# A four-layer graph network: layer-norm statistics made where rows are finished, high parts on GpSimd, GRU gates in fp16 parts, and two tests in place of nested ones

## Time and profile before

| | us |
|---|---|
| median of 3 runs | 3095.23 (3094.25 to 3100.11) |
| profiled execution | 3090.32 |
| its span, first to last instruction | 3088.6 |

### The profile page before, as it was taken

One profiled execution on the slowest core, in us unless ns is written; L12 is line 12 of the kernel. 1 busy time (PEld: TensorE's weight loads), 2 busy tenths in 40 slices (PEclk: granted clock), 3 DMA queues, 4 the chain that ended last, 5 costly groups with the idle time before them and its releaser, 6 DMA issues. The chain is left out here.

```text
span 3088.6 us, 44367 instructions
## 1 busy us (share of the span) xinstructions
PE 2345.9 (76%) x14134; PEld 1718.8 (56%) x14134; DVE 1944.9 (63%) x4750; ACT 1263.5 (41%) x2067; POOL 545.7 (18%) x1539
## 2 busy tenths in 40 slices
PE   3499999759455999987834975779545299999999
PEld 2377777558323877776512754657444144444458
DVE  5467667433437777776238778887883677777741
ACT  4455655231346666661256754667412200000000
POOL 0000000000014444340025543445300000000000
PEclk9699999879777999998956987889877599999999
DMA  1322122035100000000100000000003000000013
GB/s 44 115 94 94 73 90 75 5 127 196 43 16 6 23 24 19 25 23 16 44 17 5 15 11 10 11 15 16 10 10 111 40 1 0 0 0 0 0 48 93
DMA packets 49249, 120.82 MB, mean 39 GB/s; under 512 B 5904, under 2 KB 24624, under 8 KB 45744
## 3 DMA queue, kind: packets, MB, share of 16 engines
q1 hardware_dynamic: 49072, 118.83, 11.5%
HBM read 93.85 MB, written 24.97 MB: 38 GB/s over the span
## 5 line engine op out<-in xcount | busy, mean ns | idle before, releaser
L1823 DVE SCALAR_TENSOR_TENSOR fil_acc<-bank,fil_node,fil_acc 128x256 f32<-128x256 f32 x682 | 329.9, 484 | 110.3 <-PE bank L1891 97.6
L1285 PE MATMUL bank<-idf,X 128*128 128x128 f32 x968 | 137.1, 304 | 215.7 <-DVE step_recips L1750 215.7
L1362 ACT ACTIVATE step_PT<-bank 128x512 f32<-128x512 f32 (+1 forms) x264 | 128.2, 574 | 380.5 <-PE bank L1285 380.1
L1889 PE MATMUL bank<-parts_in,fil_xTh 128*128 128x512 f16 x704 | 268.3, 381 | 0.0
L1890 PE MATMUL bank<-parts_in,fil_xTh 128*128 128x512 f16 x704 | 268.0, 381 | 0.0
L1891 PE MATMUL bank<-parts_in,fil_xTl 128*128 128x512 f16 x704 | 267.8, 380 | 0.0
L1295 PE MATMUL bank<-kH,qHL 128*128 128x512 f16 (+1 forms) x264 | 104.4, 396 | 193.4 <-ACT step_E L1371 149.3
L1285 PEld LDWEIGHTS bank<-idf,X 128*128 128x128 f32 x968 | 121.5, 156 | 227.6 <-DVE step_recips L1750 219.1
L672 PE MATMUL bank<-V,HL 128*128 128x256 f32 x968 | 236.7, 386 | 0.2
L1317 PE MATMUL bank<-H,step_PT 128*128 128x256 f32 x968 | 216.0, 379 | 0.0
L1317 PE MATMUL bank<-A,step_PT 128*128 128x256 f32 x968 | 216.0, 379 | 0.0
(11 more groups left out here) (365 smaller groups left out, 5061.1 us busy)
## 6 DMA issues: line engine op xcount, KB each, us to landing
gat_A<-in_adj SPq DMA_DIRECT2D x22, 1408.0 KB, 6.0
step_a<-adjT SPq DMA_DIRECT2D x44, 352.0 KB, 3.0
gcn_raw<-in_L_W SPq DMA_DIRECT2D x16, 512.0 KB, 4.8
split<-gcn_halves SPq DMA_DIRECT2D x16, 512.0 KB, 3.4
parts_in<-split SPq DMA_DIRECT2D x4, 2048.0 KB, 19.4
adjT<-gat_a SPq DMA_DIRECT2D x22, 352.0 KB, 2.2
gcn_a<-adjT SPq DMA_DIRECT2D x22, 352.0 KB, 3.9
out_a<-adjT SPq DMA_DIRECT2D x22, 352.0 KB, 3.0
```

The costliest lines, as they stand in the source:

```text
L1285: last = pe.transpose(p_bank[n % nb][:, i * 128:i * 128 + 128], M[j][:, (b + i) * 128:(b + i) * 128 + 128], core.idf[:])
L1362: act.activation(PT[:, b * 128:(b + m) * 128], p_bank[n % len(p_bank)][:, 0:m * 128], ACT.Copy).then_inc(pT_done, 1)
L1823: c(dve.scalar_tensor_tensor(out=acc[k][:], in0=ps, scalar=node[k][:, n:n + 1], in1=acc[k][:], op0=ALU.mult, op1=ALU.add))
L1889: pe.matmul(w_bank[n % 4][:], xTh[k][:, x], wh[:, blk], start=c == 0, stop=False)
```

## The change

- x comes by four transfers, and ln0 makes the statistics of a quarter as soon as it is there.
- Statistics live in one tile for all norms. Those for ln1 are made in the attention stage behind each updated tile, those for ln2 in the graph convolution, those for ln2b (19 of 22) at the end of step 1, those for ln3 in ln2b.
- The high part is made by GpSimd from H and a column `by`, the low part by VectorE in one operation from H, `by` and the high part; the small buffers go.
- In ln2b, GpSimd adds the shift b to x ahead of VectorE, which scales, adds and makes the statistic for ln3.
- The gate weights and the features are split into fp16 high and low parts; each float32 product becomes three fp16 products (high by high, low by high, high by low), scaled by 64 and scaled back where the biases are added.
- `settle` makes one test for a repair (once at most) and then one test for the ties, side by side instead of nested.

The diff, cut to its core:

```diff
+LOADS = 4
+SG = 64.0
...
-AGAIN = 2
...
+        self.stats = sb("stats", [128, T * 6])
+        self.x_loaded = [ctx.enter_context(nc.semaphore(f"x_loaded{n}")) for n in range(LOADS)]
...
-        x_loaded = nc.alloc_semaphore("x_loaded")
...
-            sp.dma_start(core.X[:].rearrange("p (t f) -> p t f", t=T),
-                         x.rearrange("(t p) f -> p t f", p=128)).then_inc(x_loaded, 16)
-            sp.wait_ge(x_loaded, 16)
+            for n in range(LOADS):
+                part = slice(T * n // LOADS, T * (n + 1) // LOADS)
+                sp.dma_start(core.X[:].rearrange("p (t f) -> p t f", t=T)[:, part, :],
+                             x.rearrange("(t p) f -> p t f", p=128)[:, part, :]).then_inc(core.x_loaded[n], 16)
...
-        stats = sb("stats", [128, T * 6])
+        stats = core.stats
...
-        u = [sb(f"u{k}", [128, D]) for k in range(2)]
+        by = sb("by", [128, T])
...
-            def statistics(t, k):
-                dve.bn_stats(cols(stats, t, 6), cols(src, t)).then_inc(sem["stats_done"], 1)
-
-            pipelined(dve, [(0, statistics)])
-            dve.wait_ge(sem["stats_done"], T)
+            if parts:
+                if scale_rows is None:
+                    dve.memset(by[:], SH).then_inc(sem["by_ready"], 1)
+                else:
+                    dve.tensor_scalar(by[:], scale_rows[:], SH, None, ALU.mult).then_inc(sem["by_ready"], 1)
+                dve.wait_ge(sem["by_ready"], 1)
+            for n in range(LOADS):
+                if loading:
+                    dve.wait_ge(core.x_loaded[n], 16)
+                for t in range(max(counted, T * n // LOADS), T * (n + 1) // LOADS):
+                    dve.bn_stats(cols(stats, t, 6), cols(src, t)).then_inc(sem["stats_done"], 1)
+            if counted < T:
+                dve.wait_ge(sem["stats_done"], T - counted)
...
-            def split(t, k):
-                reuse(dve, sem["lo_done"], t)
-                dve.wait_ge(sem["rows_done"], t + 1)
-                if scale_rows is None:
-                    dve.tensor_scalar(u[k][:], cols(H, t), SH, None, ALU.mult).then_inc(sem["scaled"], 1)
-                else:
-                    dve.tensor_scalar(u[k][:], cols(H, t), cols(scale_rows, t, 1), SH,
-                                      ALU.mult, ALU.mult).then_inc(sem["scaled"], 1)
-
             def low(t, k):
                 dve.wait_ge(sem["hi_done"], t + 1)
-                dve.tensor_tensor(lo(HL, t), u[k][:], hi(HL, t), ALU.subtract).then_inc(sem["lo_done"], 1)
+                dve.scalar_tensor_tensor(out=lo(HL, t), in0=cols(H, t), scalar=cols(by, t, 1), in1=hi(HL, t),
+                                         op0=ALU.mult, op1=ALU.subtract)
 
             def scale_and_add(t, k):
                 dve.wait_ge(sem["rows_done"], t + 1)
-                c = Chain(dve, sem["affine_steps"], t * 2)
-                c(dve.tensor_tensor(cols(H, t), cols(H, t), gb[0][:], ALU.mult))
-                c(dve.tensor_tensor(cols(H, t), cols(H, t), gb[1][:], ALU.add))
-                dve.tensor_tensor(cols(X, t), cols(X, t), cols(H, t), ALU.add)
+                dve.wait_ge(sem["shifted"], t + 1)
+                dve.tensor_tensor(cols(H, t), cols(H, t), gb[0][:], ALU.mult).then_inc(sem["affine_steps"], 1)
+                dve.wait_ge(sem["affine_steps"], t + 1)
+                dve.tensor_tensor(cols(X, t), cols(X, t), cols(H, t), ALU.add).then_inc(sem["added"], 1)
+
+            def count(t, k):
+                dve.wait_ge(sem["added"], t + 1)
+                dve.bn_stats(cols(stats, t, 6), cols(X, t)).then_inc(sem["x_counted"], 1)
 
             if affine:
                 dve.wait_ge(sem["affine_loaded"], 48)
-                pipelined(dve, [(0, scale_and_add)])
+                dve.wait_ge(sem["aggregated"], T)
+                pipelined(dve, [(0, scale_and_add), (1, count)])
+                dve.wait_ge(sem["x_counted"], T)
             if parts:
-                pipelined(dve, [(0, split), (1, low)])
+                pipelined(dve, [(0, low)])
+
+        if affine:
+            @block.gpsimd
+            def _(pool):
+                pool.wait_ge(sem["affine_loaded"], 48)
+
+                def shift(t, k):
+                    pool.tensor_tensor(cols(X, t), cols(X, t), gb[1][:], ALU.add).then_inc(sem["shifted"], 1)
+
+                pipelined(pool, [(0, shift)])
+
+        if parts:
+            @block.gpsimd
+            def _(pool):
+                pool.wait_ge(sem["by_ready"], 1)
+
+                def high(t, k):
+                    pool.wait_ge(sem["rows_done"], t + 1)
+                    pool.tensor_scalar(hi(HL, t), cols(H, t), cols(by, t, 1), None, ALU.mult).then_inc(sem["hi_done"], 1)
+
+                unrolled(pool, [(0, high)])
...
-            def high(t, k):
-                act.wait_ge(sem["scaled"], t + 1)
-                core.fence(act)
-                act.activation(hi(HL, t), u[k][:], ACT.Copy).then_inc(sem["hi_done"], 1)
-
-            pipelined(act, [(0, rows), (1, high)] if parts else [(0, rows)])
+            pipelined(act, [(0, rows)])
...
-        wih, whh = sb("wih", [128, 6 * D]), sb("whh", [128, 6 * D])
+        weight_parts = [[sb(f"{n}{part}", [128, 6 * D], F16) for part in "HL"] for n in ("wih", "whh")]
...
-        xT = [sb(f"xT{k}", [128, 2 * D]) for k in range(2)]
+        xH, xL = ([sb(f"x{part}{k}", [128, 2 * D], F16) for k in range(2)] for part in "HL")
+        weights = [E2[:, 0:6 * D], P[1][:, 0:6 * D]]
...
+            for i, (whole, (high, low)) in enumerate(zip(weights, weight_parts)):
+                dve.wait_ge(w_high, i + 1)
+                dve.scalar_tensor_tensor(out=low[:], in0=whole, scalar=SG, in1=high[:], op0=ALU.mult,
+                                         op1=ALU.subtract).then_inc(w_low, 1)
+            dve.wait_ge(w_low, 2)
...
+            def low_features(t, k):
+                dve.wait_ge(xT_ready, t + 1)
+                dve.tensor_tensor(xL[k][:], xt_bank[:], xH[k][:], ALU.subtract).then_inc(xL_ready, 1)
...
-                dve.tensor_tensor(rz[k][:], rz_bank[:], bi[:, 0:2 * D], ALU.add).then_inc(gates_read, 1)
-                dve.tensor_tensor(inn[k][:], n_bank[:, 0:D], bi[:, 2 * D:], ALU.add).then_inc(gates_read, 1)
-                dve.tensor_tensor(hn[k][:], n_bank[:, D:], bh[:, 2 * D:], ALU.add).then_inc(gates_read, 1)
+                dve.scalar_tensor_tensor(out=rz[k][:], in0=rz_bank[:], scalar=1 / SG, in1=bi[:, 0:2 * D], op0=ALU.mult,
+                                         op1=ALU.add).then_inc(gates_read, 1)
...
+            def statistics(t, k):
+                dve.wait_ge(updated, t + 1)
+                dve.bn_stats(cols(core.stats, t, 6), cols(X, t)).then_inc(counted, 1)
+
+            pipelined(dve, [(3, take_product), (0, mask), (1, row_scale), (7, statistics), (6, update), (4, gates),
+                            (5, candidate), (0, larger), (3, low_features), (0, probabilities)])
...
+            act.wait_ge(loaded, 64)
+            for whole, (high, _) in zip(weights, weight_parts):
+                act.activation(high[:], whole, ACT.Copy, scale=SG).then_inc(w_high, 1)
...
-                act.activation(xT[k][:], xt_bank[:], ACT.Copy).then_inc(xT_ready, 1)
+                act.activation(xH[k][:], xt_bank[:], ACT.Copy).then_inc(xT_ready, 1)
...
-                reuse(pe, xT_ready, t, buffers=1)
+                reuse(pe, xL_ready, t, buffers=1)
...
-                pe.wait_ge(xT_ready, t + 1)
-                x_hp, x_h = xT[k][:, 0:D], xT[k][:, D:]
-                times_weight(pe, rz_bank[:], x_hp, wih, 2 * D, 0, 3 * D, stop=False)
-                times_weight(pe, rz_bank[:], x_h, whh, 2 * D, 0, 3 * D, start=False)
-                times_weight(pe, n_bank[:, 0:D], x_hp, wih, D, 2 * D, 3 * D)
-                times_weight(pe, n_bank[:, D:], x_h, whh, D, 2 * D, 3 * D).then_inc(gates_ready, 1)
+                pe.wait_ge(xL_ready, t + 1)
+                core.fence(pe)
+
+                def times_parts(ps, sources, n, off):
+                    pairs = [(x[k][:, i * D:i * D + D], weight_parts[i][part]) for i in sources
+                             for x, part in ((xH, 0), (xL, 0), (xH, 1))]
+                    for m, (x, w) in enumerate(pairs):
+                        last = times_weight(pe, ps, x, w, n, off, 3 * D, start=m == 0, stop=m == len(pairs) - 1)
+                    return last
+
+                times_parts(rz_bank[:], (0, 1), 2 * D, 0)
+                times_parts(n_bank[:, 0:D], (0,), D, 2 * D)
+                times_parts(n_bank[:, D:], (1,), D, 2 * D).then_inc(gates_ready, 1)
...
-            unrolled(dve, [(0, scale), (2, add), (2, low)])
+            def statistics(t, k):
+                dve.wait_ge(added, t + 1)
+                dve.bn_stats(cols(core.stats, t, 6), cols(X, t)).then_inc(counted, 1)
+
+            unrolled(dve, [(0, scale), (2, add), (3, statistics), (2, low)])
...
+                with dve.If(raised(1) > 0):
+                    again(p, q, valid)
```

(28 more changed lines are left out.)

24 lines of the change are left out of this document (15 added, 9 removed).

## The result

| | before | after |
|---|---|---|
| median, same chip | 3097.67 us | 3042.35 us |
| profiled execution | 3090.32 us | 3042.38 us |
| its span | 3088.6 us | 3040.7 us |
| PE, DVE, ACT, POOL busy | 2345.9, 1944.9, 1263.5, 545.7 us | 2323.6, 1941.9, 1232.8, 638.9 us |

The ratio of the medians is 0.9833, with a 95% interval of 0.9819 to 0.9846. The gain is 55 us by the medians and 47.9 by the two profiled spans; 87 were forecast, and 3042 lies 2 us above the top of the range. The mean granted clock is 0.893 in both profiled executions.

The account below looks back on a forecast made before the run. TensorE was taken to bound attention and step 0, but not step 1, where it waits for VectorE. The terms -6.2 - 23.4 - 22.4 - 22.9 + 0.4 - 12.5 sum to -87.0: 3003.3 us profiled, 3008 median; range 2985 to 3040.

Parts of the forecast that it names:

- Term 3: Rows of ln0 to ln3: high parts on GpSimd make a row 0.68 us instead of 0.98, -22.4 us in four norms.
- Term 5: Checks in the diffusion steps: two short tests make skips cheaper, -11 us in step 1 and -1.5 in step 0.
- Term 2: Statistics made where rows are finished: -23.4 us in ln1, ln2 and ln3 together, costing +0.4 in the graph convolution.
- Term 6: Affine norm ln2b: start set by the x transfer, shift on GpSimd; 0 us, bounds -4 and +5.
- Terms 1 and 4: Input by four transfers in ln0, -6.2 us; GRU gates in fp16 parts in the attention stage, -22.9 us.
- (a): Norm rows: GpSimd and VectorE take turns, so the high parts save nothing; 3030 us, chance 0.14.
- (c): Checks of step 1: two tests mean two long skips, some +18 us instead of -11; 3037 us, chance 0.12.
- (b): Attention stage: the gates give nothing because late low parts make TensorE wait; 3026 us, chance 0.07.
- (d): Step 1: a check needing a second repair goes to the exact search, +123 us; 3131 us, chance 0.04.

Follow-up runs that it names:

- the other run: The changed kernel with no statistics made ahead, every norm taking the 22 of its rows itself: 3055.3 us in one execution, 13.0 more than the changed kernel.

## Why the prediction was right or wrong

**Term 3, high parts on GpSimd, failed**, and it makes most of the miss. It put a row at 0.68 us, from GpSimd's copies of the same shape (0.34 back to back) and 0.1 for a column as scalar. The instruction takes 0.90 by itself, 2.6 times the copy it was priced from. Which of the three differences makes it so (the operation, the scalar per partition, the fp16 result) was not separated. Forecast -22.4; the table shows +1.9 in the four rows stretches, so 24.3 of the 39 us that are missing. The outcome lies at the lower bound of the term, nothing gained, and 1.9 us beyond it. The rule weighed there (the Trainium skill, "SBUF — State Buffer", Who interferes with whom) does not explain it, since the duration stayed the same without VectorE. In ln2b the trace agrees with it in direction: VectorE's addition of two SBUF operands took 0.83 and 0.74 us beside GpSimd's instead of 0.43, and the statistic with one operand stayed at 0.41.

**Term 5, the tests: right for ties and repairs, wrong for the plain check.** The step that failed is the skip of the ties' body at 0.5 us, "which is about as long in the code". The exact search lies behind the ties, inside the same skip, and the jump over both pays 1.6 us more (3.7 instead of 2.1). On VectorE the gaps behind step 1's checks fell by 9.5 us in sum where 12.8 was forecast, and the step by 4.6 where 11 was. So "most of it goes on" failed too: from one plain check to the next the kernel takes up to 1.1 us longer than before, though the gap itself grew by 0.1 only, and why stays open. Beside that, the term had no place of the code in it: step 0 lost 3.3 us, and was 5.0 shorter again when the code moved by 72 instructions.

**Term 2, the statistics: oversized in the graph convolution.** The step that failed is "again the last tile's, +0.4". A norm's statistics, unrolled as the changed kernel has them, take 7.29 us (8.00 in the loop of before, so 0.7 a norm came from the form alone). Moved, they cost 2.5 in the convolution (4.0 in the other run). This grows from tile to tile: the first addition of a result comes 0.2 us later with them, the last 1.9. Why is not shown. In the attention stage the loop hides them, as forecast. Behind it 2.2 us show (7.3 less 5.1), of which 1.7 are the gates at the lower clock; measured against the kernel before, with the gates whole in both, the stretch with them is 9.2 shorter for the 7.8 forecast. In step 1 the 19 statistics hide, as forecast.

**Term 6, ln2b: start right, pace wrong.** The transfer sets the start, but GpSimd's addition slowed VectorE's, which the term had seen and set at zero: ten rows at 1.73 us and the rest at 1.25, against 1.41 before, and a start 1.0 later behind the issue. With the statistics of term 2 the stretch came out at -4.7 instead of -7.8.

**Terms 1 and 4 were right.** The input gave 6.7 us for 6.2, of which the four transfers are 5.3 and the rest came with one transfer too. The gates gave 24.7 for 22.9: 3.9 us a tile for 4.0, VectorE not in the way.

The misses by stretch add up: 24.3 (rows), 2.6 (convolution), 4.8 and 6.4 (steps), 3.1 (ln2b), 1.8 (features, filters), less 3.2 (attention) and 0.7 (the rest) give 39.1, the difference of 87.0 and 47.9. Of the rivals, (a) named the time of the rows but not their cause, (c) applied to the plain check alone, in that it stayed at one long skip's 3.7 and did not double; (b) and (d) did not occur.

## What to carry to other kernels

Price an operation on an engine by a row of that operation with those types, not by the nearest copy; where there is none, the far bound deserves the larger chance. Work moved away from a busy engine should first be offered to the engine that is fastest at it and waits anyway: here VectorE idled 0.4 us of each 0.9 for a result it could have made in 0.35. Where an engine's program has loops and far jumps, compare two forms of the code at more than one place in the program before a few microseconds are believed.

## What was unexpected of the hardware

- The same scaling of 128x256 f32 to fp16 by a column took 0.90 us on GpSimd, 0.50 on ScalarE and 0.35 on VectorE.
- VectorE operations of 0.42 us that don't wait for each other start every 0.34 us.
- A skipped body costs 2.1 or 3.7 us in all behind two tests and 1.3 or 3.6 behind one, by the place and the length of the code, and 32 instructions without work, put in ahead of a loop, turned gaps of 11.9 us in it into one of 4.2.
- TensorE's clock rose 11.5 us behind a stage's first load in one kernel and 16.5 in another whose stage is the same, and the matmuls took 3.2 us longer.
- 72 counts on a semaphore that VectorE makes alone took 6.4 us, 0.09 each.
